# Moving the inverse deviation of the MLP stage's layer norms from VectorE to GpSimd

## The reference

```
residual = x
h = layer_norm(x, n1_g, n1_b)                 # over the 128 channels
h = irfft2(block-diagonal filter(rfft2(h))) + h + residual
residual = h
h = layer_norm(h, n2_g, n2_b)                 # (h - mean) * rsqrt(var + 1e-5) * g + b
h = gelu(h @ mw1 + mb1)                       # 128 -> 512
return h @ mw2 + mb2 + residual               # 512 -> 128
```

## Time and profile before

| what | value |
|---|---|
| time, median of 3 executions | 1784.01 us (1781.05 to 1790.11) |
| time of the profiled execution | 1787.48 us |
| its span, first to last instruction | 1785.7 us |
| TensorE busy in the span | 92% |
| VectorE busy | 67% |
| ScalarE busy | 52% |
| GpSimd busy | 35% |
| mean granted TensorE clock | 0.977 |

### The profile page before, as it was taken

One profiled execution on the slowest core, in us unless ns is written; L12 is line 12 of the kernel. 1 busy time (PEld: TensorE's weight loads), 2 busy tenths in 40 slices (PEclk: granted clock), 3 DMA queues, 4 the chain that ended last, 5 costly groups with the idle time before them and its releaser, 6 DMA issues.

```text
span 1785.7 us, 35087 instructions
## 1 busy us (share of the span) xinstructions
PE 1636.1 (92%) x11184; PEld 1453.6 (81%) x11184; DVE 1195.5 (67%) x2880; ACT 934.6 (52%) x1778; POOL 630.5 (35%) x756
## 2 busy tenths in 40 slices
PE   0099989999999998999999998999999999899999
PEld 0088878888889887888889887888888988688888
DVE  7959956666646976666664895666664697566663
ACT  4335426666634534666652452666663453466665
POOL 4800004777750001677781000477775000111111
PEclk9999989999998998999998999999999999999999
DMA  8210061333320033333330006133332003211111
GB/s 246 100 54 1 1 220 59 101 105 105 100 80 1 1 115 117 103 103 106 106 101 24 1 1 220 54 97 103 106 107 84 1 1 126 77 36 31 34 36 48
DMA packets 164896, 138.85 MB, mean 78 GB/s; under 512 B 9186, under 2 KB 127332, under 8 KB 164804
## 3 DMA queue, kind: packets, MB, share of 16 engines
q1 hardware_dynamic: 164516, 137.15, 24.0%
q10 hardware_dynamic: 288, 0.46, 0.1%
HBM read 70.47 MB, written 67.11 MB: 77 GB/s over the span
## 4 chain that ended last, share of the span: by engine, by line
PE 44%; DVE 21%; POOL 17%; issue 15%; ACT 1%; DVEq 1%; DMA 1%; SPq 0%; POOLq 0%; ACTq 0%
PE ps L641 13%; PE ps L496 7%; PE ps L590 6%; POOL arena L1191 6%; POOL gz L1160 4%; DVE vsb L942 4%; POOL gz L1164 4%; PE ps L632 4%; PE ps L634 3%; PE ps L633 3%; DVE csb L944 3%; DVE usb L931 3%; DVE usb L932 2%; POOL arena L1198 2%; PE ps L621 2%
## 5 line engine op out<-in xcount | busy, mean ns | idle before, releaser
L641 PEld LDWEIGHTS ps<-mw,gel 128*128 128x128 f32 x4096 | 533.2, 191 | 43.3
L641 PE MATMUL ps<-mw,gel 128*128 128x128 f32 x4096 | 536.4, 274 | 0.0
L751 ACT ACTIVATE gel<-ps,mb1f 128x512 f32<-128x512 f32 x512 | 351.6, 687 | 269.9 <-PE ps L634 238.7
L1198 POOL TENSOR_TENSOR arena<-arena,mb2rep 128x512 f32<-128x512 f32 x128 | 163.5, 1277 | 886.0 <-ACT hn L737 886.0
L632 PE MATMUL ps<-hth,mw1h 128*128 128x512 f32 x512 | 262.9, 513 | 8.1 <-DVE htl L1024 7.8
L1191 POOL TENSOR_SCALAR arena<-xnext,rstd,shift 128x128 f32<-128x128 f32 x384 | 168.4, 457 | 217.7 <-DVE shift L1127 217.7
L737 ACT ACTIVATE hn<-arena,shift,rstd 128x128 f32 (+1 forms) x512 | 221.6, 482 | 35.6 <-DVE shift L1127 35.6
L1007 DVE TENSOR_TENSOR arena<-ps,arena 128x512 f32 (+1 forms) x64 | 44.2, 691 | 266.0 <-PE ps L613 241.9
L496 PE MATMUL ps<-cst,arena 128*128 128x128 f32 x1024 | 130.2, 294 | 90.3 <-DVE arena L904 81.4
L634 PE MATMUL ps<-hth,mw1l 128*128 128x512 f32 x512 | 204.4, 399 | 0.0
L496 PEld LDWEIGHTS ps<-cst,arena 128*128 128x128 f32 x1024 | 129.4, 208 | 90.8 <-DVE arena L904 81.5
(11 more groups left out here) (92 smaller groups left out, 2428.8 us busy)
## 6 DMA issues: line engine op xcount, KB each, us to landing
arena<-aside SPq DMA_DIRECT2D x128, 256.0 KB, 5.0
aside<-gz SPq DMA_DIRECT2D x96, 256.0 KB, 3.0
between<-xout SPq DMA_DIRECT2D x62, 256.0 KB, 2.3
xnext<-between SPq DMA_DIRECT2D x62, 256.0 KB, 3.0
out_dram<-xout SPq DMA_DIRECT2D x62, 256.0 KB, 2.3
aside<-first SPq DMA_DIRECT2D x32, 256.0 KB, 2.0
xnext<-in_x_dram SPq DMA_DIRECT2D x31, 256.0 KB, 3.0
mw1raw<-in_L_mw_dram SPq DMA_DIRECT2D x4, 256.0 KB, 2.5
```

The source lines that it names most:

```text
L641: mm = pe.matmul(ps[:, r % 2, P * i:P * i + P], gel[:, r % 2, m, P * i:P * i + P], mw2[:, m, :], start=(m == 0 and i == 0), stop=(m == CHU ...
L751: act.activation(gel[:, r % 2, m, :], ps[:, 2 + m % 2], ACT.Gelu, bias=mb1f[:, m:m + 1]).then_inc(gelu_out, 1)
L1198: pool.tensor_tensor(t, t, b, ALU.add).then_inc(mb2_done, 1)
```

## The change

GpSimd computes the inverse deviation as the power of variance plus epsilon to minus one half, and the shift. VectorE only takes the statistics and raises a new semaphore `st_done`. GpSimd's new function `inverse` runs at every even tile, ahead of `z_rows`.

```
-                        if known >= 2:
-
-                            dve.wait_ge(hn_done, TILES * s + 2 * q - 2)
                         h2(s, i, h)
...
+                    if known >= 2 and (main or nxt):
+                        dve.wait_ge(rs_done, RS * s + q - 1)
                     if main:
                         dve.wait_ge(h2_done, TILES * s + 2 * q + 2)
...
-                    if nxt and known >= 4:
-
-                        dve.wait_ge(z_new, TILES * s + 2 * q - 6)
...
                     if main or nxt:
-                        own.add(ins)
-                        own.settle()
-                        a, b = 0 if main else 2 * ROWS, 4 * ROWS if nxt else 2 * ROWS
-                        inverse_std(dve, own, stats[:, h, a:b, 2], var[:, a:b], rstd[:, h, a:b], nt0[:, a:b])
-                        dve.scalar_tensor_tensor(shift[:, h, a:b], stats[:, h, a:b, 1], -1.0, rstd[:, h, a:b],
-                                                 ALU.mult, ALU.mult).then_inc(rs_done, 1)
+                        ins.then_inc(st_done, 1)
...
+            def inverse(s, q, main, nxt):
+
+                h = q % 2
+                a, b = 0 if main else 2 * ROWS, 4 * ROWS if nxt else 2 * ROWS
+                pool.wait_ge(st_done, RS * s + q + 1)
+                if main and q >= 2:
+                    pool.wait_ge(hn_done, TILES * s + 2 * q - 2)
+                if nxt and q >= 4:
+                    pool.wait_ge(z_new, TILES * s + 2 * q - 6)
+                own.add(pool.tensor_scalar(var[:, a:b], stats[:, h, a:b, 2], 1.0 / C, LN_EPS, ALU.mult, ALU.add))
+                own.add(pool.tensor_scalar(negmean[:, a:b], stats[:, h, a:b, 1], -1.0, None, ALU.mult))
+                own.settle()
+                own.add(pool.tensor_tensor(rstd[:, h, a:b], var[:, a:b], neghalf[:, a:b], ALU.pow))
+                own.settle()
+                pool.tensor_tensor(shift[:, h, a:b], negmean[:, a:b], rstd[:, h, a:b], ALU.mult).then_inc(rs_done, 1)
...
+                    q = n // 2
+                    if n % 2 == 0 and (q < PAIRS or nxt):
+                        inverse(s, q, q < PAIRS, nxt and q >= LAG)
                     if again:
                         h0 = ROWS * tile_of(j - 1, r)
                         pool.wait_ge(rs_done, RS * s + 2 * j + r // 2 + 1)
```

More of the change, by code:

```diff
@@ L208, in afno @@
         var = sb("var", [P, 4 * ROWS])
-        nt0 = sb("nt0", [P, 4 * ROWS])
+        negmean = sb("negmean", [P, 4 * ROWS])
+        neghalf = sb("neghalf", [P, 4 * ROWS])
         gz0 = sb("gz0", [P, ROWS, C])
@@ L270, in afno @@
         mlp_w, mlp_b_mm, mlp_b = sem("mlp_w"), sem("mlp_b_mm"), sem("mlp_b")
-        iw_mm, h2_done, rs_done = sem("iw_mm"), sem("h2_done"), sem("rs_done")
+        iw_mm, h2_done, st_done, rs_done = sem("iw_mm"), sem("h2_done"), sem("st_done"), sem("rs_done")
         hn_done, t_mm, hi_out, lo_out = sem("hn_done"), sem("t_mm"), sem("hi_out"), sem("lo_out")
@@ L280, in afno @@
         resid_in = [sem(f"resid_in{i}") for i in range(3)]
-        dve_own = sem("dve_own")
+        dve_own, pool_own = sem("dve_own"), sem("pool_own")
         source = [x[0], x[1], between[0], between[1]]
@@ L1143, in _ @@
                 with dve.Fori(2, PAIRS // 2 - 1) as i:
-                    own.enter(i, 2 * 14, 2)
+                    own.enter(i, 2 * 2, 2)
                     for h in range(2):
@@ L1156, in _ @@
         def _(pool):
+            own = Chain(pool, pool_own)
+            def inverse(s, q, main, nxt):
[12 more added lines that the diff above has]
+                pool.tensor_tensor(shift[:, h, a:b], negmean[:, a:b], rstd[:, h, a:b], ALU.mult).then_inc(rs_done, 1)
+            own.add(pool.memset(neghalf[:, :], -0.5))
             def scale(s, h0, tmp):
```

## The result

After the change the kernel takes 1804.63 us (median of 4 executions, 1802.89 to 1809.8) against 1787.06 us before (4 executions, 1781.05 to 1790.13): ratio 1.011, 95% interval 1.0084 to 1.0135. The profiled execution takes 1802.89 us, span 1801.1, so 15.4 us more than the span before.

The account below looks back on a forecast made before the run. TensorE was taken to bound the middle, a chain through VectorE the ramps, GpSimd's last `z_rows` the ends. Ramps -3.9 and ends -0.3 made -4.2 us, from 1784.0 to 1779.8; range 1773 to 1800.

Parts of the forecast that it names:

- the power's price: GpSimd's time for one power, shown by no row: chosen as 1.0 us at width 16, 0.55 at width 8.
- The rest of `inverse`: Hand-off, small instructions and waits on GpSimd around the power, from statistics' end to first `z_rows`: 0.95 us.
- the low end: Rival for ramps and ends: the power is a plain 0.20 us instruction and nothing collides; sum -10.4, 1774 us, chance 0.12.
- The power is a long routine: Rival at the ends of steps 0 to 2: the change is slower, +16 us, 1800; chance 0.20.
- c16: Time of one `inverse` at width 16, from statistics' end to first `z_rows` instruction: forecast 1.95 us.
- c8: Time of one `inverse` at width 8, in the ramp and at the end: forecast 1.5 us.
- The end: Ends of steps 0 to 2: one chain saved, two paid; +0.2, -0.7 and +0.2 us, together -0.3.
- The ramp: Start of the MLP stage in four steps: shorter chain and no low-part delay, less the collision; 3.9 us gained.
- The collision: In the ramp, GpSimd's `inverse` stalls beside VectorE's instructions: between 0 and 1.2 us, taken as 0.4.
- The middle: Pairs under a full TensorE, 15.28 us each: the added GpSimd work costs nothing.
- the cover: GpSimd's idle time in a middle pair, 4.10 us; beyond it each further us costs some 42 us.
- Not on the path: Rival: something beside the chain holds the ramp, so its gain vanishes and the ends stay; 1784 us, chance 0.10.

Follow-up runs that it names:

- e1: Changed kernel with a product in place of the power, so the inverse deviation is not computed: 1776.56 us, ratio to the kernel before 0.9959.
- e6: Changed kernel with VectorE waiting for the first pair's inverse before it splits the MLP weights: 1802.07 us in one execution.
- e3: Changed kernel with the chains of pairs 0, 1, 16 and 17 back on VectorE's Newton series: 1790.64 us, ratio 1.0034 to the kernel before.
- e7: Changed kernel with the power taken twice, with the same result: 1944.19 us in one execution.
- e11: Kernel before with GpSimd's last rows first, SyncE's last stores first and the weight products in two halves behind pairs 14 and 15: 1766.08 us, ratio 0.9902.
- e12: Changed kernel with GpSimd's last rows first and SyncE's last stores first, weight products not moved: 1774.83 us, ratio 0.9952 to the kernel before.

## Why the prediction was wrong

**The step that failed is the choice of the power's price.** "I choose 1.0 at width 16 and 0.55 at width 8" between 0.20 and 3.1 / 1.6. It measured 2.93 and 1.67, close to the upper bound at width 16 and 0.07 above it at width 8. The bound, eleven instructions at GpSimd's pace, was a better guess than my reason for leaving it, that a power is more than one plain operation and fewer than three Newton steps: that compares counts of operations, not of time. The rest of `inverse`, forecast at 0.95, measured 4.07 - 2.93 = 1.14 and 2.77 - 1.67 = 1.10.

The 2.6 cycles an element that the Trainium skill (GPSIMD Engine Reference, section 3.1) gives for two inputs led to the low end, 1774; for a power the rows disagree by far (158 ns a value, where the 512 elements of `scale` cost 1.30 us in all, 2.5 ns each), and they agree only for plain operations, of which alone that section speaks.

**The rival was right, and underrated.** "The power is a long routine" had a chance of 0.20 and this account: c16 = 4.05, c8 = 2.55, ends 4.4, 4.4 and 3.5, ramps 1.1 or 0.7 lost each, +16 in sum. Measured: c16 = 4.07, c8 = 2.77, ends +4.9, +4.9 and +4.0, ramps +0.7, +0.5, +0.7, +0.7, and 15.4 us in the span. Its point of decision, a power of 2.6 us, is passed. e1 shows that the power alone makes the sign. Its time, 1800, came out low by 4.6: 3.1 of them because it was put on the first median of the kernel before, 1784.0, where four executions gave 1787.06, and the rest because the medians stand 17.6 us apart instead of 16.

**The end.** The formula 2 x c8 + max(0, c16 - 1.06) - 3.70 gives 5.54 + 3.01 - 3.70 = 4.85 with the measured values; the rows show 4.9. The mechanism was right: one chain saved, two paid, and the lateness of pair 15's pass on top. The 0.9 us of cover at the turn of layers held too (4.9 - 0.9 = 4.0).

**The ramp.** Step 0: 2.42 becomes 3.32, less the 0.22 for the low part, makes +0.68; the table has +0.73. The collision was counted at 0.4 and measured 0.6 (e6), within its bounds. In step 1 the low part's delay of 0.67 should have been saved, which makes 3.32 - 2.42 - 0.67 = +0.23; the table has +0.54. The rows show that the delay was saved (the low part starts 0.03 us behind the high part), but that TensorE's four transposes took 0.95 us instead of 0.65: in 691.12:692.07 of the changed kernel the mean granted clock is 0.62, in 688.45:689.10 of the kernel before 1.00. In step 2 they take 1.11 us at 0.50 instead of 0.66. The forecast had no term for the clock.

**The middle.** "Cost nothing" is right: 236.97 us in each step. But it was right by 0.03 us of GpSimd's time a pair, and in that paragraph I had named only the period as what suffers once the cover is gone. The cover pays for something else before: a longer `inverse` delays GpSimd's last pass of the middle, which is the 3.0 us in the end's formula, and in e3 VectorE's own chain takes some 1.2 us more through stalls. Beyond the edge, e7 confirms the forecast of some 42 us for each further us a pair: 2.97 us cost 123.3, that is 41.5 for each.

**Not on the path.** This rival is refuted: ramps and ends both moved with the duration of `inverse`, in e1 one way and in the changed kernel the other.

## What to carry to other kernels

When work is moved to an idler engine and its price is unknown, price the longest routine first and ask which stretch it decides; where the sign hangs on that one number, the chance of the far end must not be a remainder. An engine that only just fits under the bound of a loop costs nothing in it, but comes out of it with its last pass unfinished, and pays at the end of the stage. When an end waits for one engine's queue, look at every queue behind it before reordering: here the wait went from GpSimd to SyncE's stores and to VectorE's weights, and of the three variants of the kernel before only the one with all three orders brought 1% (SyncE's order without the moved weights was tried on the changed kernel alone, where it took the ratio from 1.0037 to 0.9952). A closed gap can also give back clock behind it.

## What the runs showed of the hardware

- A power on GpSimd took 2929 ns at 128x16 and 1666 at 128x8, by estimate 158 ns a value on a partition and about 0.4 us fixed; a product of the same shapes 222 and 204 ns.
- VectorE and GpSimd can block each other for whole instructions, in both directions. GpSimd's `negmean` went from 0.24 to 0.75 us beside VectorE's L992 (0.75 us); VectorE's small instructions go from 0.17 to 1.2 us beside GpSimd's additions (1.27). The Trainium skill (SBUF — State Buffer, section "SBUF: two separate sides") calls it an exclusive lock, and these rows agree. Not every pair of instructions collides: beside the power of 1.67 us at 262.24 VectorE's `h2`, which adds from PSUM (L1016, 262.64), took its usual 0.68.
- The granted clock is at its lower level around the gaps at the ends. In the kernel before TensorE idles for 4.43 us and the clock is at 0.50 from 511.90 to 518.70; in the changed kernel TensorE idles for 9.33 us and it is at 0.50 from 517.30 to 524.10, 2.85 us of it in `dft_w`. In e11 and e12, with gaps of at most 0.25 us ahead of the `dft_w` of steps 1 and 3, these take 30.3 and 30.4 us at 1.00.
- The stretch from `dft_w` to the MLP stage's statistics takes 163.4 to 166.5 us in some steps and about 168.5 in others, in both kernels, and which step has which differs between the two profiled executions. It goes with the granted clock just behind `dft_w`. Busy time by stretch (columns as in the earlier trace rows), first the kernel before, steps 1 and 3, then the changed one, step 1 and step 3:

```profile
547.00:580.00 33.00, 32.44 (x199) 29.48 (x198) 22.80 (x54) 15.50 (x32) 0.00 (x0) 0.84 0.01 1
1399.00:1432.00 33.00, 32.37 (x233) 29.17 (x232) 26.46 (x61) 17.11 (x36) 0.00 (x0) 1.00 0.00 1
```

```profile
553.00:586.00 33.00, 32.36 (x233) 29.20 (x232) 26.61 (x61) 17.16 (x36) 0.00 (x0) 1.00 0.00 1
1409.00:1442.00 33.00, 32.43 (x212) 29.60 (x211) 23.92 (x55) 16.03 (x33) 0.00 (x0) 0.90 0.00 1
```

At 0.84 TensorE is as busy as at 1.00, with 199 products instead of 233 in the same 33 us. So profiled executions differ by 4 to 5 us a step in a stretch in which the change has no instruction; e1's is shorter by 9.5 us for it (165.5 / 164.4 / 164.3 / 164.9), though whether e1's other values have a part in that is not shown. I take it for part of the spread of the runs and of the 2.2 us by which the medians differ more than the spans, but what decides between the two lengths was not tried and stays open.
